# Post-norm decoder block on one core: half-width score products, a reordered attention prologue and a two-product low-rank tail

## The reference, cut to what matters

```python
# state-space mixer: 8 groups of 1024 channels; gated group output, then
g = y * silu(gate)
gg = gg * rsqrt(mean(gg * gg) + EPS)          # per group
out = (gg * norm_w) @ out_proj_w.T
# cross attention, 32 query heads over 8 key heads of 128
kv = concatenate([context, latents], axis=1)
q = rms_norm(latents @ Wq, q_norm_w); k = rms_norm(kv @ Wk, k_norm_w); v = kv @ Wv
out = softmax(q k.T / sqrt(128)) v @ Wo
# last sublayer: dense layer with a low-rank part, chosen per batch, and a shared one
y = x @ kernel + bias + (x @ A_eff.T) @ B_eff.T + (x @ A_shared.T) @ B_shared.T
```

## Time and profile before

| | |
|---|---|
| median of 3 runs | 2495.38 us (2494.32 to 2496.31) |
| the profiled execution | 2494.62 us, of which the span of instructions is 2492.9 us |
| busy: PE, DVE, ACT, POOL | 98%, 74%, 46%, 45% of the span |
| mixer's groups | about 249 to 1623 us |
| cross attention | from 1636 us |
| last sublayer's batches | from 2448 us |

### The profile page before, as it was taken

The page is one execution under the profiler, slowest core; times in us unless marked ns, Lnnn a source line. Parts: engine busy times, 40 slices in busy tenths (PEclk is TensorE's granted clock), DMA queues, the critical chain, the costliest instruction groups (busy, mean ns, idle before and its releaser), DMA issues. The chain is left out here.

```text
span 2492.9 us, 39413 instructions
## 1 busy us (share of the span) xinstructions
PE 2449.8 (98%) x14024; PEld 2025.1 (81%) x14024; DVE 1841.1 (74%) x2568; ACT 1157.9 (46%) x2732; POOL 1134.0 (45%) x928
## 2 busy tenths in 40 slices
PE   8999999999999999999999999989999999999999
PEld 5667788888888888888888888878888888888886
DVE  4798995986976967958869869666667666766674
ACT  3444433443443443433433433555566566666551
POOL 5332765555655655555556456643223223223123
PEclk9999999999999999999999999999999999999999
DMA  5100431321412313204203113111011011111100
GB/s 185 60 26 30 165 111 44 126 93 56 145 45 89 123 34 119 98 30 148 98 34 145 67 64 115 60 43 35 26 29 50 23 30 48 29 28 31 53 3 34
DMA packets 71622, 172.64 MB, mean 69 GB/s; under 512 B 9312, under 2 KB 17632, under 8 KB 63008
## 3 DMA queue, kind: packets, MB, share of 16 engines
q1 hardware_dynamic: 64448, 165.37, 19.1%
q10 hardware_dynamic: 7008, 4.98, 0.6%
HBM read 165.08 MB, written 5.24 MB: 68 GB/s over the span
## 5 line engine op out<-in xcount | busy, mean ns | idle before, releaser
L295 PE MATMUL pair<-XH,d_w_hi 128*128 128x512 f32 x1160 | 471.8, 407 | 1.9 <-DVE d_gated L1893 1.7
L296 PE MATMUL pair<-XL,d_w_hi 128*128 128x512 f32 x1160 | 460.0, 397 | 0.0
L297 PE MATMUL pair<-XH,d_w_lo 128*128 128x512 f32 x1160 | 459.4, 396 | 0.0
L1737 POOL TENSOR_TENSOR d_decay<-d_decay,d_cb 128x1024 f32<-128x1024 f32 x128 | 315.4, 2466 | 134.5 <-DVE d_decay L1870 123.6
L1870 DVE TENSOR_TENSOR_SCAN d_decay<-d_decay,m_delta 128x1024 f32<-128x1024 f32 x128 | 361.1, 2822 | 1.8 <-DVE d_dtg L1838 1.3
L1718 POOL TENSOR_TENSOR d_w_lo<-d_w,d_w_hi 128x512 fp32r<-128x512 f32 x144 | 190.9, 1328 | 259.3 <-ACT d_w_hi L1536 258.6
L295 PEld LDWEIGHTS pair<-XH,d_w_hi 128*128 128x128 f32 x1160 | 218.6, 188 | 59.5 <-issue 11.7
L1855 DVE SCALAR_TENSOR_TENSOR d_hs<-pair,d_conv,d_hs 128x1016 f32<-128x1016 f32 (+2 forms) x192 | 242.9, 1265 | 29.3 <-ACT d_hs L1561 24.8
L297 PEld LDWEIGHTS pair<-XH,d_w_lo 128*128 128x128 f32 x1160 | 218.5, 188 | 52.9
L296 PEld LDWEIGHTS pair<-XL,d_w_hi 128*128 128x128 f32 x1160 | 218.8, 189 | 47.3 <-issue 0.2
L1561 ACT ACTIVATE d_hs<-pair,d_conv 128x1024 f32<-128x1024 f32 x64 | 77.2, 1206 | 360.7 <-PE pair L297 360.7
(11 more groups left out here) (305 smaller groups left out, 6120.6 us busy)
## 6 DMA issues: line engine op xcount, KB each, us to landing
d_decay<-token_decays SPq DMA_DIRECT2D x64, 1024.0 KB, 4.9
d_w<-in_L_w_groups SPq DMA_DIRECT2D x144, 256.0 KB, 2.6
e_w<-in_L_w_heads SPq DMA_DIRECT2D x80, 256.0 KB, 2.7
d_wo<-in_L_wo_groups SPq DMA_DIRECT2D x64, 256.0 KB, 5.0
e_ctx<-in_ctx_t SPq DMA_DIRECT2D x8, 512.0 KB, 9.5
context_keys<-k_out SPq DMA_DIRECT2D x9, 256.0 KB, 2.1
X<-in_x SPq DMA_DIRECT2D x8, 256.0 KB, 10.3
b_ctx<-in_ctx SPq DMA_DIRECT2D x8, 256.0 KB, 11.6
```

Of the source, the lines that this page charges most:

```text
L295: pe.matmul(out, wh, xh, start=first, stop=False)
L296: pe.matmul(out, wh, xl, start=False, stop=False)
L297: return pe.matmul(out, wl, xh, start=False, stop=last)
L1737: pool.tensor_tensor(r, r, GM_[:], ALU.mult).then_inc(q["scores"], 1)
```

## The change

Four edits. (1) In the mixer, the `scores` of the next group's first item become four products of half the width, at batches 2, 3 (first head) and 4, 5 (second head). (2) In the attention prologue ACT and DVE wait for the norm weights later; ACT computes one exponential of a constant column before `q_sq(1)`; unit 2's `k_var`, `v_lo`, `k_norm` and `q_copy` move ahead of `softmax_sum(0)` on DVE, its `k_power` ahead of one weight rest on POOL, its `q_sq` ahead of two weight copies on ACT, and its `q_var` behind `softmax_max(1)`. (3) In the last sublayer MID and BT are split into fp32r parts: MID's hi in rows 0 to 63 and its lo in rows 64 to 127, BT's hi in both halves, BT's lo in the upper rows only with zeros below, so that two fp32r matmuls of 128 rows give hi*hi + lo*hi + hi*lo. ACT writes each per-batch BT part twice, DVE makes the rests. (4) POOL adds the biases of the batches earlier and writes the zeros.

```diff
@@ mixer, POOL
+                def first_scores(g, e, h):
+                    if h == 0:
+                        pool.wait_ge(q["cb"], START + g + 1)
+                        pool.wait_ge(q["decay"], START + 2 * g * JT + e + 1)
+                    t = tokens(h)
+                    done = pool.tensor_tensor(R[:, 0, e, t], R[:, 0, e, t], GM_[:, t], ALU.mult)
+                    if h == 1:
+                        done.then_inc(q["scores"], 1)
...
-                        if not last_group and b in (2, 3):
-                            scores(g + 1, 0, b - 2)
+                        if not last_group and 2 <= b < 6:
+                            first_scores(g + 1, b // 2 - 1, b % 2)
@@ attention, SP
-                sp.wait_ge(q["kv_proj"], U)
-                for x in range(2):
-                    sp.dma_start(BT[RL:, x, :], a["L1_ffn_bs_t"]).then_inc(fq["bt_in"], 16)
+                sp.wait_ge(q["w_split"], HK * NI)
+                for part in shared(BS):
+                    sp.dma_start(part, a["L1_ffn_bs_t"]).then_inc(fq["bt_in"], 16)
@@ PE, base
-                    pe.wait_ge(fq["mid"], b + 1)
-                    pe.wait_ge(fq["bt"], b + 1)
-                    pe.matmul(bank[:, :], MID[:, b % 2, :], BT[:, b % 2, :], start=False, stop=True)\
+                    pe.wait_ge(fq["bt_lo"], b + 2)
+                    pe.wait_ge(fq["mid_lo"], b + 1)
+                    pe.matmul(bank[:, :], MID[:, b % 2, :], BTL[:, b % 2, :], start=False, stop=False)
+                    pe.matmul(bank[:, :], MID[:, b % 2, :], BTH[:, b % 2, :], start=False, stop=True)\
@@ ACT, prologue
-                act.wait_ge(q["const"], 16)
                 evac_kv(0)
                 q_sq(0)
                 evac_kv(1)
+                act.wait_ge(q["const"], 16)
                 k_hi(0)
...
                 evac_kv(2)
+                act.activation(FIRST_EXP[:], c.mhalf[:, 0:1], ACT.Exp)
                 q_sq(1)
...
                 exp(0)
+                q_sq(2)
                 e.w_hi(act, 8)
                 e.w_hi(act, 9)
-                q_sq(2)
@@ ACT, last sublayer
+                act.wait_ge(fq["bt_in"], 32)
+                for hi, raw in zip(shared(BTH), shared(BS)):
+                    act.activation(hi, raw.rearrange("r (o d) -> r o d", o=1).broadcast_to([RL, 2, D]), ACT.Copy)\
+                       .then_inc(fq["bs_hi"], 1)
                 turned(4, 5)
...
-                    act.activation(BT[0:RL, b % 2, :], c.bank[4 + b // 4][(b % 4) * RL:(b % 4 + 1) * RL, :],
-                                   ACT.Copy).then_inc(fq["bt"], 1)
+                    for x in (0, R2):
+                        act.activation(BTH[x:x + RL, b % 2, :], bt_rows(b), ACT.Copy).then_inc(fq["bt_hi"], 1)
@@ POOL
+                k_power(2)
                 e.w_lo(pool, 7)
-                k_power(2)
...
                 f_w_lo(0, 1)
+                bias(0)
                 norm_rstd(c, pool, s, 5)
                 f_w_lo(2, 3)
+                bias(1)
...
+                pool.tensor_tensor(BTL[:].rearrange("p x (k n) -> p (x k) n", n=P), one, one, ALU.subtract)\
+                    .then_inc(fq["zeros"], 1)
                 norm_rstd(c, pool, s, 6)
+                bias(2)
+                bias(3)
                 norm_rstd(c, pool, s, 7)
-                for b in range(3):
+                for b in (4, 5, 6, 7):
                     bias(b)
@@ DVE, last sublayer
+                def bt_lo(b):
+                    v.wait_ge(fq["bt_hi"], 2 * b + 2)
+                    v.tensor_tensor(BTL[0:RL, b % 2, :], bt_rows(b), BTH[0:RL, b % 2, :].bitcast(F32),
+                                    ALU.subtract).then_inc(fq["bt_lo"], 1)
+                    v.wait_ge(fq["mid_hi"], b + 1)
+                    v.tensor_tensor(MID[R2:, b % 2, :], low_bank(b), MID[0:R2, b % 2, :].bitcast(F32),
+                                    ALU.subtract).then_inc(fq["mid_lo"], 1)
...
+                bs_lo()
+                bt_lo(0)
                 for b in range(NB):
+                    if b + 1 < NB:
+                        bt_lo(b + 1)
```

More of the change, by code:

```diff
@@ L2075, in stage_cross_attention @@
         AL = e.place("f_a_lo", [P, KD, NB, R2], F32R, "decay", 2 * KD * D + KD * NB * R2)
-        BT = e.place("f_bt", [R2, 2, D], F32, "kv")
-        MID = e.place("f_mid", [R2, 2, S], F32, "kv", 2 * D)
+        BTH, MID = e.place("f_bt_hi", [P, 2, D], F32R, "kv"), e.place("f_mid", [P, 2, S], F32R, "kv", 2 * D)
+        BTL, BS = e.place("f_bt_lo", [P, 2, D], F32R, "hs"), e.place("f_bs", [P, D], F32, "hs", 2 * D)
         c.sems = c.sems + e.sems
@@ L2080, in stage_cross_attention @@
         s = NormSems(c, "e")
-        fq = sems(c, "f_", "la_in mix_in w_in bt_in mix w_hi w_lo at_hi at_lo am am_hi am_lo bt_ready bt low_ready mid "
-                           "out_ready biased stored")
+        fq = sems(c, "f_", "la_in mix_in w_in bt_in mix w_hi w_lo at_hi at_lo am am_hi am_lo bs_hi zeros bt_ready bt_hi bt_lo "
+                           "low_ready mid_hi mid_lo out_ready biased stored")
         fs = NormSems(c, "f")
@@ L2087, in low_bank, with shared, bt_rows @@
             return c.bank[6 + b % 2][0:R2, 0:S]
+        def shared(t):
+            return [t[x + RL:x + R2] for x in (0, R2)]
+        def bt_rows(b):
+            return c.bank[4 + b // 4][(b % 4) * RL:(b % 4 + 1) * RL, :]
         def am_bank(k):
@@ L2113, in kept @@
             return None
-        KEPT = sb("e_kept", [P, 2, HD])
+        KEPT, FIRST_EXP = sb("e_kept", [P, 2, HD]), sb("e_first_exp", [P, 1])
         kept_in = [c.sem(f"e_kept_in{i}") for i in range(2)]
@@ L2263, in low @@
                     if b >= 2:
-                        pe.wait_ge(fq["mid"], b - 1)
+                        pe.wait_ge(fq["mid_lo"], b - 1)
                     pe.wait_ge(s.lo, b + 1)
@@ L2376, in q_sq @@
                     ahead(act, "negmax", n - 1)
+                    if n == 2:
+                        act.wait_ge(q["exp"], GQ)
                     for h in range(GQ):
@@ L2482, in _ @@
                         act.wait_ge(fq["out_ready"], b - 1)
-                    act.activation(BT[0:RL, b % 2, :], c.bank[4 + b // 4][(b % 4) * RL:(b % 4 + 1) * RL, :],
-                                   ACT.Copy).then_inc(fq["bt"], 1)
+                    for x in (0, R2):
+                        act.activation(BTH[x:x + RL, b % 2, :], bt_rows(b), ACT.Copy).then_inc(fq["bt_hi"], 1)
                     act.wait_ge(fq["low_ready"], b + 1)
-                    act.activation(MID[:, b % 2, :], low_bank(b), ACT.Copy).then_inc(fq["mid"], 1)
+                    act.activation(MID[0:R2, b % 2, :], low_bank(b), ACT.Copy).then_inc(fq["mid_hi"], 1)
                     if b == 1:
@@ L2537, in _ @@
                 f_w_lo(0, 1)
+                bias(0)
                 norm_rstd(c, pool, s, 5)
                 f_w_lo(2, 3)
+                bias(1)
+                pool.wait_ge(q["w_split"], HK * NI)
+                one = c.ident[:].rearrange("p (o n) -> p o n", o=1).broadcast_to([P, 2 * D // P, P])
+                pool.tensor_tensor(BTL[:].rearrange("p x (k n) -> p (x k) n", n=P), one, one, ALU.subtract)\
+                    .then_inc(fq["zeros"], 1)
                 norm_rstd(c, pool, s, 6)
+                bias(2)
+                bias(3)
                 norm_rstd(c, pool, s, 7)
-                for b in range(3):
+                for b in (4, 5, 6, 7):
                     bias(b)
                 for b in range(NB):
-                    if b + 3 < NB:
-                        bias(b + 3)
                     norm_rstd(c, pool, fs, b)
@@ L2653, in f_at_lo, with bs_lo @@
                          .then_inc(fq["at_lo"], 1)
+                def bs_lo():
+                    v.wait_ge(fq["bs_hi"], 2)
+                    v.wait_ge(fq["zeros"], 1)
+                    v.tensor_tensor(shared(BTL)[0], shared(BS)[0].rearrange("r (o d) -> r o d", o=1)
+                                    .broadcast_to([RL, 2, D]), shared(BTH)[0].bitcast(F32), ALU.subtract)\
+                     .then_inc(fq["bt_lo"], 1)
+                def bt_lo(b):
[5 more added lines that the diff above has]
+                                    ALU.subtract).then_inc(fq["mid_lo"], 1)
                 def am_lo(k):
@@ L2666, in _ @@
                 k_var(1)
+                v.wait_ge(q["const"], 16)
                 k_lo(0)
@@ L2673, in _ @@
                 q_var(1)
+                k_var(2)
                 k_lo(1)
                 q_lo(1)
-                softmax_sum(0)
-                k_var(2)
                 v_lo(2)
@@ L2680, in _ @@
                 q_copy(2)
-                q_var(2)
+                softmax_sum(0)
                 for n in range(U - 3):
                     softmax_max(n + 1)
+                    if n == 0:
+                        q_var(2)
                     k_lo(n + 2)
```

3 lines of the change are left out of this document (removed).

## The result

| | before | after |
|---|---|---|
| median of 6 executions each, timed together | 2495.51 us | 2478.35 us |
| lowest to highest | 2494.32 to 2496.31 | 2476.78 to 2478.74 |
| the profiled execution, its span | 2494.62, 2492.9 us | 2477.92, 2476.2 us |

The ratio is 0.9931 (95%: 0.9918 to 0.9944): 17.2 us less, where 13.6 were predicted.

A forecast was written before the change was run, and what follows sets the result against it. TensorE, busy 98% of the span, was taken to bound the kernel. Gains of 3.1 + 0 + 5.5 + 5.0 = 13.6 us gave 2494.62 - 13.6 + 0.4 = 2481.4 us, range 2478.5 to 2485.0.

The forecast's parts named there:

- Edit 1: Mixer: first item's scores in halves let POOL's gated_lo end earlier, removing seven PE waits; gain 3.1 us.
- Edit 2: Attention prologue: ACT and DVE wait later for the norm weights; gain 0, up to 1.4 us without project_kv(2)'s cover.
- Edit 3: Attention prologue: exponential's table load moves into ACT's gap ahead of q_sq(1), so exp(0) starts 1.3 us earlier.
- Edit 4: Attention prologue: behind the shorter wait for exp(0), score(1) and the turns run at full clock; gain 1.4 us.
- Edit 5: Attention prologue: unit 2's work moved up leaves 0.3 of PE's 3.08 us wait for k_lo(2); gain 2.8 us.
- (a): Attention prologue: the clock drops all the same behind the shorter wait; +1.1, 2482.5 us; chance 0.15.
- Edit 6: Last sublayer: two fp32r passes replace the fp32 product, saving 0.69 us for each of 8 batches; net 5.0 us.
- (b): Last sublayer: rests come late in every batch, each product by some 0.35 us; +2.8, 2484.2 us; chance 0.12.
- (c): Mixer: POOL's halves save nothing, the waits move to batches with new work; +3.1, 2484.5 us; chance 0.08.
- (d): Attention prologue: table load doesn't fit ACT's 1.52 us gap, exp(0) not earlier; +2.7, 2484.1 us; chance 0.05.
- (e): PE stays at the low clock after dropping at the stage's boundary, slower than before; 2501 us; chance 0.02.
- (f): Anywhere: something unseen takes nearly all the gain, within 0.2%; 2492 us; chance 0.03.

The follow-up runs named there:

- second trace of before: The kernel before, unchanged, timed as if it were a change and traced again: 2494.13 us, ratio 1.0000.

## Why the prediction was right or wrong

**Edit 1, 3.1 us: mechanism right, size wrong.** The failing step is "PE, 0.46 us late now" and "7 * 0.45". By the starts of the rows a wait cost 0.57 to 0.60 us, and by the mixer's length (4.3 to 4.6 us less) 0.61 to 0.65, 4.4 us in all. The bracket of idle time starts at the modelled end of a short matmul (0.28 us for a row of two that cost 0.14 us); a wait has to be priced by starts, as the front part says of matmuls in general. The upper bound of 3.1 us was no bound for the same reason. This is 1.3 of the 3.05 us by which 2478.35 us lies under the predicted 2481.4. (The gains differ by more, 17.2 against 13.6, since before's median came out 0.5 us above the 2495.0 that the prediction subtracts from.)

**Edit 2, 0: right for the profiled execution, but not in general.** With a low stretch at the boundary it is worth nothing, as its undoing shows. Without one it is worth 0.55 us, within the "up to 1.4 us" that the prediction named "if that cover were gone"; four of the 14 traces are of this kind.

**Edit 3, 1.3 us: right.** The load stands in the gap, the exponential of a column is 0.20 us as taken, and undone it lengthens the wait by 1.44 us. The page that spoke against the edit (the Trainium skill, "ScalarE: Activation LUTs", "What ACT_TABLE_LOAD costs") has a drain of 1.38 us beside the load. In these rows the load follows `v_hi(2)` (1636.74 and 0.39 us) by 0.01 us and `q_sq(1)` follows the exponential by 0.02: the drain isn't there, and the measurement decides.

**Edit 4, 1.4 us: wrong.** The failing step is "the low clock costs 1.42 us". It compared unit 0's stretch with unit 2's and took the difference for clock. The second trace of before shows 2.97 us for that stretch at the full clock: a wait of 1.03 us for `k_norm(2)` was hidden under the low clock. In the profiled execution the low stretch cost 0.1 us, so in the kernel before taking it away was worth 0.1. With edit 5 in place, where nothing but 0.56 us is left to hide it, it costs 0.7 us (the kernel without edit 3): what it is worth depends on the other edits.

**Edit 5, 2.8 us: too small by just this.** 3.9 us, since it removes the hidden wait too. Edits 3 and 5 together are 5.3 us, and 5.5 were predicted for 3 to 5: the sum came from two starts, 1659.07 - 1653.6, and was right to 0.2 us although its split was wrong.

**The clock outside the one trace: missing.** The prediction forecast that of the two slow stretches the second goes and the one at the boundary stays, and priced both by where they lay in one execution. In the other two traces of before the second lies where PE pays for it in full, 1.5 us. So the profiled execution of before had 1.5 us less of that cost than the other two and 1.7 us more at the start of the kernel, and both together looked like a normal time. So the failing step is to take one execution of before as the base of the 5.5 us: in the mean of three traces each, attention gains 6.8 us, 1.3 us more. The spans' means gained 17.0 us, 3.4 more than the sum of 13.6: 1.3 of edit 1, 1.3 of attention, 0.6 by chance in unchanged code (0.3 us ahead of the mixer, 0.3 at 263 us) and 0.1 of the last sublayer. The low end of the range allowed some 1.3 us for the case that the boundary's stretch "falls elsewhere", which happened in one of three traces of after, but nothing for a base that moves. The Trainium skill ("TensorE: Matmul & The Clock Gate", "Part 1: The HAM clock gate") says that the monitor runs freely and doesn't restart with a kernel. The traces agree so far: the wait of 2.00 us at the boundary is the same to 0.01 us in all 14 traces, and ten of them have a low stretch behind it, four have none. The prediction cited this and used it only for rival (a), not for the base that it subtracted from.

**Edit 6, 5.0 us: right.** 5.1 us in the traces, 4.6 in the timing of it alone. The first batch's wait was priced at 0.35 us and stands as 0.44, which by starts (2440.94 to 2441.77, less 0.23) is 0.60.

**Rivals.** (a) isn't seen: no low stretch behind a wait of 0.9 us in any of the seven traces that have one of 0.4 to 0.95 us there, or in the one with unit 2 put back. (b) isn't seen: one wait for `f_mid`, at batch 0. (c) isn't seen: PE has no wait for `gated_lo` left. (d), (e) and (f) aren't seen either: the load fits its gap, and a low stretch in the prologue cost 1.5 us at most. Every rival made the gain smaller. None was a mechanism by which the kernel could gain more than the sum, and that is the side on which the time came out.

## What to carry to other kernels

Price a wait by the distance between the starts of PE's rows, against the same pair without a wait, and not by the idle time in brackets. A stretch at the low clock has a price only where nothing behind it waits anyway, so compare two executions before giving it one; and a wait that lies under a low stretch shows only in an execution without it. Where the clock is in play, shortening waits can pay twice, once for the wait and once for the low stretches that no longer follow it. The second part, 0.9 us by the traces here, shows only in the mean over executions.
